# Attention phase: VectorE's normalisations, low part of hT and weighting at other places of a sequence, GpSimd's score sums one unit later

## The reference, cut to what matters

```python
x = x + 0.5 * ffn(layernorm(x))          # mixture of experts, top 2 of 8
x = x + attn(layernorm(x))
x = x + 0.5 * ffn(layernorm(x))

def attn(x):                             # 32 sequences of 256 tokens, D = 128, 16 heads of 64
    x = x + linear_attention(layernorm(x) * g1 + b1)
    h = layernorm(x) * g2 + b2
    return x + gelu(h @ Wf1) @ Wf2

def linear_attention(x):
    Q, K, V = phi(x @ Wq), phi(x @ Wk), x @ Wv          # phi = elu + 1, by heads
    num[t] = sum over t' <= t of (Q[t] . K[t']) V[t']
    den[t] = sum over t' <= t of (Q[t] . K[t'])
    return (num / den) @ Wo
```

## Time and profile before

| | |
|---|---|
| time, median of 3 runs | 1941.07 us (1940.9 to 1946.44) |
| span of the profiled execution | 2011.4 us |
| TensorE busy in the span | 1704.0 us (85%) |
| VectorE busy | 1581.6 us (79%) |
| ScalarE busy | 1073.7 us (53%) |
| GpSimd busy | 967.7 us (48%) |

### The profile page before, as it was taken

One profiled execution on the slowest core, in us unless ns is written; L12 is line 12 of the kernel. 1 busy time (PEld: TensorE's weight loads), 2 busy tenths in 40 slices (PEclk: granted clock), 3 DMA queues, 4 the chain that ended last, 5 costly groups with the idle time before them and its releaser, 6 DMA issues. The chain is left out here.

```text
span 2011.4 us, 36431 instructions
## 1 busy us (share of the span) xinstructions
PE 1704.0 (85%) x12528; PEld 1385.0 (69%) x12528; DVE 1581.6 (79%) x4382; ACT 1073.7 (53%) x1937; POOL 967.7 (48%) x1010
## 2 busy tenths in 40 slices
PE   4356899983999999999999999999999957799990
PEld 2245677863778777777777777777777745677770
DVE  7667797764888888988888888898888636688784
ACT  2134577763555556555565555655556424577670
POOL 4866501115544464555546546445553324566661
PEclk9999899996999999999999999999999967899995
DMA  7554467740000010010001001001000004576657
GB/s 244 181 208 159 164 247 260 267 156 16 12 9 9 8 21 17 9 20 19 12 16 20 16 12 21 17 9 20 18 12 11 12 11 179 173 244 228 224 196 265
DMA packets 90512, 188.15 MB, mean 94 GB/s; under 512 B 14893, under 2 KB 52442, under 8 KB 79322
## 3 DMA queue, kind: packets, MB, share of 16 engines
q1 hardware_dynamic: 43434, 126.93, 18.6%
q0 software_dynamic: 33840, 46.17, 8.6%
q10 hardware_dynamic: 13056, 12.72, 1.8%
HBM read 131.08 MB, written 54.69 MB: 92 GB/s over the span
## 5 line engine op out<-in xcount | busy, mean ns | idle before, releaser
L1643 POOL TENSOR_TENSOR at_sc<-at_sc 128x512 f32<-128x512 f32 x128 | 198.1, 1548 | 344.7 <-DVE at_sc L1743 344.5
L569 ACT ACTIVATE f_hid<-f_up_ps,f_w 128x512 f32<-128x512 f32 x312 | 213.7, 688 | 184.5 <-PE f_up_ps L433 130.1
L1735 DVE SCALAR_TENSOR_TENSOR at_qk<-at_exps,at_relus 128x512 f32<-128x512 f32 x256 | 182.8, 715 | 100.1 <-ACT at_relus L1552 97.4
L1743 DVE TENSOR_TENSOR at_sc<-at_s_ps,mask 128x384 f32<-128x384 f32 x512 | 251.6, 549 | 1.1 <-PE at_s_ps L1376 1.1
L973 DVE TENSOR_TENSOR f_hid_lo<-f_hid,f_hid_hi 128x512 fp32r<-128x512 f32 x312 | 209.4, 688 | 16.0 <-ACT f_hid_hi L576 6.7
L689 POOL DMA_INDIRECT expert_rows<-f_rows_out,f_dest x156 | 167.7, 1075 | 98.1 <-DVE f_rows_out L1001 61.1
L2050 POOL DMA_INDIRECT x<-finished_rows,slot x120 | 195.7, 1631 | 29.7 <-issue 29.7
L1616 ACT ACTIVATE raw<-at_num_ps 128x512 f32<-128x512 f32 x128 | 76.1, 595 | 241.4 <-PE at_num_ps L1413 220.5
L672 POOL DMA_INDIRECT sent_rows<-f_xn,slot x144 | 147.5, 1024 | 74.3 <-issue 40.6
L1373 PE MATMUL at_s_ps<-at_qk 64*128 64x256 f32 x1024 | 171.0, 411 | 7.2 <-issue 5.6
L1551 ACT ACTIVATE at_exps<-at_proj_ps 128x512 f32<-128x512 f32 x253 | 152.4, 602 | 35.9 <-PE at_proj_ps L1351 29.1
(11 more groups left out here) (349 smaller groups left out, 4836.0 us busy)
## 6 DMA issues: line engine op xcount, KB each, us to landing
f_w<-split_weights SPq DMA_DIRECT2D x78, 1028.0 KB
f_got<-sent_rows SPq DMA_DIRECT2D x78, 264.0 KB
finished_rows<-f_rows_out POOLq DMA_DIRECT2D x39, 256.0 KB, 2.9
split_weights<-f_split SPq DMA_DIRECT2D x8, 1024.0 KB
sent_rows<-f_pads ACTq DMA_DIRECT2D x16, 264.0 KB
x<-in_L_attn_x SPq DMA_DIRECT2D x16, 256.0 KB, 3.9
raw<-in_L_ffn_we SPq DMA_DIRECT2D x16, 256.0 KB
out_x<-x ACTq DMA_DIRECT2D x16, 256.0 KB, 4.5
```

The costliest lines, as they stand in the source:

```text
L569: A(hid[:, c, :], up_bank(n)[:, :], ACT.Silu, bias=w[:, i % RING_W, 4 * HID + c:4 * HID + c + 1].bitcast(FP32)).then_inc(s_silu, 1)
L1643: g.tensor_tensor(sc[:, n % RING_SC, :, 3, :], sc[:, n % RING_SC, :, 1, :], sc[:, n % RING_SC, :, 2, :], ALU.add).then_inc(s_sum, 1)
L1735: stt(full, exps[:, p % 2, :], 1.0, relus[:, p % 2, :], ALU.min, ALU.add).then_inc(s_phi, 1)
L1743: last = tt(flat(sc[:, (n // 2) % RING_SC, 2 * (n % 2) + half, 0:3, :]), s_ps[2 * (n % 2) + half][:, 0:3 * P], flat(mask[:, :, :]), ALU.mult)
```

## The change

In VectorE's queue, per round (ahead: sequence s+2 exists; rest: s-1 has its rest to do):

- `normalise("A")` and `stats("B")` go from behind the masks of unit 1 to ahead of them, right behind the unit's first `phi`; `normalise("B")` in unit 2 likewise.
- `hT_low` goes from unit 3 to unit 0 of the next round, behind `weigh(s, 0)`.
- In unit 1, `weigh(s, 3)`, `find_slots` and the first half of the routing go ahead of the second `phi`; `aggregate("B")` comes before `stats("D")`, `aggregate("D")` into unit 1.
- `normalise_for_router` and `make_base` go from the end of unit 3 to unit 2, ahead of the step that makes `a_nat`.
- Behind `a_nat`, `stats("C")`, `aggregate("C")`, the sum `xa`, half of the routing and `normalise("C")` follow one another in unit 2; the second `phi` of unit 2 comes behind them. Before, `normalise("C")` stood at the start of unit 3, behind that `phi`.

In GpSimd's queue:

- `sum_blocks(n)` is taken at unit u for n = 4s + u, one unit later than before, and has a new wait: in unit 1 for `normalise("A")`, in unit 2 for `normalise("B")`, else for the unit's first `phi`.
- the inverse of D goes from unit 2 to unit 1; in the draining rounds the transfers of `send` go from unit 1 to unit 2, behind the inverse of C.

The queues of TensorE, ScalarE and SyncE are the same, row by row.

```diff
             def sum_blocks(n):
+                s, u = n // UNITS, n % UNITS
                 pool.wait_ge(s_masked, 2 * n + 2)
+                if u == 1 and has_z(s):
+                    pool.wait_ge(s_y, s + 3)
+                elif u == 2 and has_z(s):
+                    pool.wait_ge(s_z, s + 3)
+                elif ("qk", n + 2, 1) in number:
+                    pool.wait_ge(s_phi, 2 * (n + 2) + 2)
...
-                    n = UNITS * s + u + 1
-                    if n < LAST:
-                        sum_blocks(n)
+                    if UNITS * s + u < LAST:
+                        sum_blocks(UNITS * s + u)
...
-                    if u == 2 and ends_routed(s):
+                    if u == 1 and ends_routed(s):
                         inverse_std("D", s - 1)
...
-                    if u == 1 and placed_in(s) is not None and s >= NB:
+                    if u == 2 and placed_in(s) is not None and s >= NB:
                         send(placed_in(s), 0)
```

More of the change, by code:

```diff
@@ L1670, in _ @@
             add_back(2, 0)
-            sum_blocks(0)
             add_back(2, 1)
@@ L1884, in _ @@
                     g = UNITS * s + u
-                    if u == 3 and rest:
-                        normalise("C", s, lambda q: an[:, q, :], lambda q: a_nat[:, q, :], s_an)
                     if ("qk", g + 2, 1) in number:
                         phi(2 * (g + 2) + 1)
+                    if u == 1 and ahead:
+                        normalise("A", s + 3, lambda q: y[:, (s + 2) % NRING, q, :], lambda q: k.x[:, xc(s + 2, q)], s_y)
+                        dve.wait_ge(s_y, s + 3)
+                        stats("B", lambda q: y[:, (s + 2) % NRING, q, :])
+                    if u == 2 and ahead:
+                        normalise("B", s + 3, lambda q: z[:, q, :], lambda q: y[:, (s + 2) % NRING, q, :], s_z)
                     if g + 1 < LAST:
@@ L1914, in _ @@
                         weigh(s, 0)
+                    if u == 0 and s >= 1 and has_z(s - 1):
+                        hT_low(s + 1)
                     if u == 1 and down:
@@ L1918, in _ @@
                         tt(k.x[:, xc(s - 2)], slot_ps[:, 0:BT], flat(xa[:, :, :]), ALU.add).then_inc(s_x, 1)
+                    if u == 1 and ahead:
+                        dve.wait_ge(s_st["B"], s + 3)
+                        aggregate("B")
                     if u == 1 and ends_routed(s):
@@ L1921, in _ @@
                         stats("D", lambda q: k.x[:, xc(s - 2, q)])
-                    if u == 1 and ahead:
-                        normalise("A", s + 3, lambda q: y[:, (s + 2) % NRING, q, :], lambda q: k.x[:, xc(s + 2, q)], s_y)
-                        dve.wait_ge(s_y, s + 3)
-                        stats("B", lambda q: y[:, (s + 2) % NRING, q, :])
                     if u == 1 and rest:
                         weigh(s, 2)
+                    if u == 1 and ends_routed(s):
+                        dve.wait_ge(s_st["D"], s - 1)
+                        aggregate("D")
+                    if u == 1 and placed is not None:
+                        find_slots(placed)
+                    if u == 1 and choosing is not None:
+                        dve.wait_ge(s_so_far, 1)
+                        for i in (1, 2, 3):
+                            route(choosing, i)
+                    if u == 1 and rest:
+                        weigh(s, 3)
                     if u == 2 and has_hidden(s):
@@ L1930, in _ @@
                     if u == 2 and ends_routed(s):
-                        dve.wait_ge(s_st["D"], s - 1)
-                        aggregate("D")
-                    if u == 2 and ahead:
-                        normalise("B", s + 3, lambda q: z[:, q, :], lambda q: y[:, (s + 2) % NRING, q, :], s_z)
+                        normalise_for_router(s - 2)
+                        make_base(s - 2)
                     if u == 2 and rest:
@@ L1939, in _ @@
                         stats("C", lambda q: a_nat[:, q, :])
+                        dve.wait_ge(s_st["C"], s)
+                        aggregate("C")
+                        tt(flat(xa[:, :, :]), flat(a_nat[:, :, :]), k.x[:, xc(s - 1)], ALU.add).then_inc(s_xa, 1)
+                    if u == 2 and choosing is not None:
+                        for i in (4, 5, 6):
+                            route(choosing, i)
+                    if u == 2 and rest:
+                        normalise("C", s, lambda q: an[:, q, :], lambda q: a_nat[:, q, :], s_an)
                     if u == 3 and rest:
@@ L1943, in _ @@
                         tt(h2_lo[:, :], h2[:, :], h2_hi[:, :].bitcast(FP32), ALU.subtract).then_inc(s_h2_lo, 1)
-                    if u == 3 and ahead:
-                        hT_low(s + 2)
                     if u == 3 and has_hidden(s):
                         router_silu(s - 3)
-                    if u == 2 and rest:
-                        dve.wait_ge(s_st["C"], s)
-                        aggregate("C")
                     if ("qk", g + 3, 0) in number:
@@ L1957, in _ @@
                         weigh(s, 1)
-                    if u == 1 and ahead:
-                        dve.wait_ge(s_st["B"], s + 3)
-                        aggregate("B")
-                    if u == 1 and rest:
-                        weigh(s, 3)
-                    if u == 1 and placed is not None:
-                        find_slots(placed)
-                    if u == 1 and choosing is not None:
-                        dve.wait_ge(s_so_far, 1)
-                        for i in (1, 2, 3):
-                            route(choosing, i)
-                    if u == 2 and rest:
-                        tt(flat(xa[:, :, :]), flat(a_nat[:, :, :]), k.x[:, xc(s - 1)], ALU.add).then_inc(s_xa, 1)
-                    if u == 2 and choosing is not None:
-                        for i in (4, 5, 6):
-                            route(choosing, i)
-                    if u == 3 and ends_routed(s):
-                        normalise_for_router(s - 2)
-                        make_base(s - 2)
 def macaron_kernel(nc, x, ln1_g, ln1_b, wq, wk, wv, wo, ln2_g, ln2_b, wf1, wf2,
```

## The result

The changed kernel takes 1912.07 us (median of 4 runs, 1911.1 to 1914.83), the kernel before 1941.29 in the same comparison (4 runs, 1940.9 to 1946.44). The ratio is 0.9839, with a 95% interval of 0.9821 to 0.9858: 29.2 us less, where 44.4 were forecast. The time lies in the range of 1868 to 1924, but outside the forecast's own 1885 to 1905, and a third of the gain is missing.

A forecast was written before the change was run, and what follows sets the result against it. TensorE was taken to set the time, with VectorE late for it once a round at each of two places. 26.7 + 13.7 + 4.0 = 44.4 us off 1941.1 gave 1896.7 us (forecast's own 1885 to 1905; stated range 1868 to 1924).

The forecast's parts named there:

- Unit 1, the broadcast: TensorE's wait at L1323 for `weigh(s, 2)`, late behind a stretched norm A, was to vanish: 26.7 us, bounds 22.2 and 27.
- The wait goes whole: Unit 1: `weigh(s, 2)` ends near 992.3, TensorE needs it at 992.88, so all 26.7 us go, 0.6 us to spare.
- `an`: Units 2 and 3: norm C's output comes before TensorE's transposes need it, saving 14 x 0.98 = 13.7 us, bounds 0 and 16.3.
- the 2.6 us of the other rounds: Part of the wait for `an`, in rounds with scatters, not counted as gain because ScalarE sees TensorE's values late there.
- The draining round: Round 32: with the inverse of C ahead of the eight scatters, `an` starts at 1639.5 instead of 1643.53, saving 4.0 us.
- the scatters end about 1650, just ahead of the closing sum: Draining round: the moved scatters would still end before the closing sum; if late, the gain is 3 us, not 4.0.
- The low part of hT: Moved to unit 0 ahead of a `phi` that waits 1.14 us for ScalarE, its 0.42 us was to cost nothing.
- norm D's end: Unit 2, ahead of `a_nat`: 1.2 us of work may meet a sum; VectorE at most 0.3 us late, taken as zero.
- the sums a unit later: GpSimd's last sum of a round comes in unit 3; denominators needing it start about 3 us later, so free.
- rival 2: Collisions only move, to `router_low`, norm D, the base or h2's low part: 1910, or 1924 with h2 late; chance 0.20.
- rival 1: More comes back: waits behind ScalarE, including 11.5 us for `at_vals`, shorten too, so 65 to 70 us go: 1873; chance 0.13.
- Rival 4: Slower: norm C waits for GpSimd and blocks VectorE's queue; with 4.1 us lateness 14.5 us slower, 1956; chance 0.06.

The follow-up runs named there:

- e1: Kernel before with GpSimd's part alone, the sums a unit later with their new waits, VectorE's queue untouched: 1980.4 us, ratio 0.991.
- e2: Changed kernel with the sums at their old places and without the new waits, so VectorE's new order alone: 1963.23 us, ratio 0.9838.
- e0: Kernel before, unchanged, run for a second trace in another comparison: 1997.6 us beside a before of 1996.4.
- e11: Kernel before with two scatters in each of units 2 and 3 of every round, four and four in the draining round: 1941.78 us, ratio 0.9991.
- e3: Kernel before with GpSimd's sums cut to 4x2 elements from 4x128, part of the arithmetic left out: 2004.45 us, ratio 1.0049.
- e7: Kernel before with norm C, the sum `xa` and half of the routing moved ahead of unit 2's second `phi`: 1982.75 us, ratio 0.9921.
- e10: Kernel before with only the draining round's eight scatters moved behind the inverse of C: 2000.34 us beside a before of 1996.07.
- e8: Changed kernel with the draining round's scatters split, four ahead of the inverse of C and four behind: 1962.86 us, ratio 0.9846.
- e5: Changed kernel, unchanged, run again in another comparison, beside a before of 1997.79 us: 1967.95 us, ratio 0.9846.
- e9: e8 with two scatters in each of units 2 and 3 of every round instead of four in every second round's: 1936.18 us, ratio 0.9703.
- e6: Changed kernel with GpSimd's sums cut to 4x2 elements from 4x128, part of the arithmetic left out: 1992.79 us, ratio 0.998.

## Why the prediction was right, and a third too high

**What bounded the kernel** was read rightly: TensorE, with VectorE late for it at two places a round.'s two waits are gone in after, and TensorE is busy 98.5% of the window, more than the 97 to 98% forecast.

**Unit 1, the broadcast, 26.7 us.** The mechanism as told, though either half of the change alone takes the wait away (e1, e2): `weigh(s, 2)` with its broadcast, ready 0.55 us ahead of need (0.6 forecast). The size was off a little. "The wait goes whole" left out who is late next: 0.96 us earlier, TensorE comes to the transposes at L1356 ahead of ScalarE's `relus` and waits 0.21 us, 28 times: 6.0 us where e0 and e11 have 0.4. e1 and e3 show the net: 0.7 us in a round without scatters, not 0.96.

**`an`, 13.7 us.** Right: e7 alone gives 1.05 us in a round without scatters and a gain of 15.0 us. It ends 0.86 us ahead of need (0.95 forecast). VectorE waits 0.88 us for the inverse of C, not 0.6, at no cost. Leaving the 2.6 us of the other rounds out was right too, in e7.

**The draining round, 4.0 us.** This is the term that was wrong in sign. `an` and the closing sum are 4 us earlier, as told. The step that failed is "the scatters end about 1650, just ahead of the closing sum; if they are late, it is 3 us". The scatters do end ahead of the closing sum, their landing too (1565.8 and 1566.2). What the step left out is GpSimd's drain of 6.6 us behind them, so that the phase ends 8.5 us behind the last record. The end grew from 37.1 to 39.5 us, 2.4 us lost in place of 4.0 won. e10 has such a loss with that edit alone (1.6), and e8 takes it back.

**The low part of hT, norm D's end, the sums a unit later: nothing.** Right. The low part of hT takes 418 ns behind a `phi` that waits. Norm D's end costs nothing although `router_low` ahead of it meets the sum and takes 2.06 us; the bound of 1.9 us was well set, and `a_nat` wasn't late. So rival 2's mechanism happened and its price didn't. The low part of h2, which rival 2 named, keeps its 412 ns. "Free" for the last sum of a round with scatters was nearly right: in after it meets the cast of the inverse denominators (L1917, 1.0 to 1.7 us in 13 rounds instead of 0.29), and in the round around 1032 TensorE starts its broadcast at 1032.84, about 0.1 us late. (The rule of the Trainium skill that the prediction drew on, "SBUF — State Buffer", section "Who interferes with whom", named the low parts as at risk and the masks not. The trace of after agrees for the router's low part, 2066 ns, and for the masks, which keep their 547; the norms of before, with one tensor from SBUF, were stretched too. The other rule that it drew on, that the later of the two is blocked, isn't borne out by the records of rows 4, though the prediction says so: the first half of that norm is recorded from 990.09 to 992.42, so it began 0.35 us ahead of the sum. Rows 4 show that VectorE stands still, and not who has to come first.)

**The sum.** Of the 44.4 us, 5.6 come back at L1356, 6.4 are the draining round, and 1.5 are the last round but one, which took 30.7 us in after and 29.2 in before but lies anywhere between 27.9 and 31.15 in kernels that don't differ there. That gives 30.9 us; measured were 29.2, between 27.6 and 34.8 by the interval. The rest of 1.7 us is within it.

**What the forecast took for the kernel's and was the execution's.** It expected rounds of 34.5 us instead of 35.9. It got 33.85 instead of 35.15 (e11), a gain of 1.3 against 1.4, from another level: the trace of before has late updates, 18.2 us of remote waits of ScalarE for instance, and a pair of its rounds takes 71.9 us where e11 has 70.3. The 11.5 us at L1349, on which rival 1 rested, belonged to them: they aren't there in e11 or in after. Where updates do come late, about half of the gain in a round with scatters is waited for again: 0.5 us (36.6 to 36.1) of the 0.96 arrive, as the prediction argued for `an` and not for the broadcast; rounds without scatters gave 1.7 instead (35.1 to 33.4). The ratio is the same in both conditions, 0.9839 and 0.9846. That the base didn't mislead the sum more is luck in part: it was taken as a difference, and its terms were waits for VectorE, which both conditions have.

**Luck in the number.** The stated range goes past the forecast's 1905 only because it takes in rival 2, at 1910 and up to 1924, and 1912 lies in that part. What rival 2 priced at 1910, `an` late and 13.7 us lost, didn't happen; losses at two other places came to about as much.

**Rival 4** found nothing: norm C waits for GpSimd 0.9 us at most.

## What to carry to other kernels

When a step becomes the last that an engine does in a phase, cost it to the point at which that engine has left the phase, not to the end of its record: here 1.4 us of landing and 6.6 of drain turned 4 won into 2.4 lost, and with four transfers ahead and four behind the end was 35.6 us, 1.5 less than before's. When a stall is taken away, go one step further along the engine that had it and ask who was hidden behind the stall: 0.21 us in each of 28 rounds were. And before a trace is used as a base, see whether its waits for "remote" are the kernel's: here it took traces of the same kernel from two comparisons (after and e5).

## What the runs showed of the hardware

- A sum on GpSimd stops VectorE in some forms and not in others: `router_low` goes from 0.44 to 2.06 us, `at_r` from 0.42 to 2.17, the norms of 0.34 to as much as 2.4; `weigh` (at 1007.51, beside the sum of 1006.30) and the masks, which read PSUM, pass it. Such a collision costs the kernel what its place costs, here 0.7 us a round at norm A and nothing at the router's.
- In some executions TensorE's signals reach the other engines late, at most 2.6 us, while GpSimd issues four scatters in a row: 49 to 68 of 1147 updates, and another 2 to 25 aren't recorded. In other executions none is late; before took 1997.79 and 1943.75 us on the same chip in two comparisons. With two scatters in a row no engine waits for such a signal (e9). With eight nearly in a row, the sum between the two groups of four made tiny, they are up to 4.3 us late, and a round with scatters costs 1.7 to 2.3 us more (e3, e6). What makes them late isn't shown.
- The last of a group of scatters has landed 1.3 to 1.4 us behind the end of its record, after four in a row as after eight. At the end of the phase GpSimd then drains for 6.6 us, in e9 and e11 for 5.8.
